# Weights in four groups in the order of need, and the first sequence's attention preparation while they arrive

## The chip, the core and the metric

The kernel runs on one core of one Trainium2 chip. The core has five engines with queues of their own: TensorE (PE), VectorE (DVE), ScalarE (ACT), GpSimd (POOL) and SyncE (SP), which here issues every DMA. They meet only at semaphores. All DMAs of a core run on the same 16 DMA engines. The metric is the device time of one execution in microseconds, lower is better; a measurement is the median of several runs.

## The reference

The input is 16 sequences of 512 tokens with 256 features. They pass four layers, each `x = x + f(layernorm(x))`: an attention, a feed-forward layer, a second attention, and a layer of decision trees. Both attentions have 16 heads of 16 features.

```
attention 0:  per key block of 256: m = max(s), e = exp(s - m); num += e @ v; den += sum(e); out = num/den; out @ w_o
ffn 0:        bitlinear(x, w): scale = clip(mean|w|, 1e-5) per output row; tern = clip(round(w/scale), -1, 1)
              forward weight = w + (tern - w), times scale
              h = bitlinear(x, w_fc) + gate * (x @ v.T @ fast_b.T @ u.T);  bitlinear(relu(h)^2, w_proj)
attention 1:  softmax(q k / 4) v with biases; out @ out_w + out_b
ffn 1:        logits = x @ W_in.T + b_in;  8 trees of 255 nodes; silu(logits) of the nodes on the path
              that the signs of the logits choose, times W_out
```

## The kernel before, in words

The sequences are worked on in 8 pairs. A pair goes through 8 phases: attention 0 of sequence 0 (phase 0) and of sequence 1 (phase 1), the feed-forward layer of both (2, 3), attention 1 of both (4, 5), and the trees of both (6, 7). Matmuls keep nearly float32 precision by splitting each factor into a high and a low float16 part and summing three products (`PRODUCTS`). So each weight is held as a high part, 64 times the weight rounded to float16, and a low part, the rest.

The order of the work is written out by hand, engine by engine, in five blocks: SP from line 260, POOL from 348, ScalarE from 471, VectorE from 659, TensorE from 963. Within a block each instruction waits for those before it. The semaphores count up over the whole kernel.

*Start-up before.* SP issues all loads (lines 262 to 265): `w_fc`, `w_proj`, small ones, the eight attention weights, `winT`, the two halves of `woutT` (127 inner nodes, 128 leaves), biases and constants; then the first two x. All of these but the last two and the x count on `w_in`, and POOL, ScalarE, VectorE and TensorE each begin with a wait for all of them (`ALL_IN`). The raw weights lie in `probs`, `oT`, `vn`, `qst` and `kst`, the buffers of attention.

- ScalarE (474 to 482): absolute values of `w_fc` and `w_proj`, a copy of the low-rank product, then the high parts of 12 weight tensors; that of `wfc` is last, since it needs the ternary weights.
- TensorE (969 to 984): means of the absolute values by matmuls with a constant, and the low-rank product.
- VectorE (662 to 707): the scales (670, 688), the ternary weights (672 to 696), ones in `vn` (698), the gated low-rank product added to `w_fc` (701), and the 12 low parts in one fused instruction each (707).

Then TensorE waits for all low parts and for `krows`, VectorE reads x, and the first sequence starts: `arrived`, `moments`, `normalise` (709 to 735), the transpositions (1004), `hT_high` and `hT_low`, `qk_unit` and `v_unit`, `qk_read`, POOL's `qk_low` (359), and SP's `stack_up` (277), 24 copies that stack high and low parts of q and k in `qst` and `kst`. Then come the row maxima of the first 7 heads (`LEAD`): a matmul into one of two PSUM banks (1040), a reduction on VectorE (753). POOL's `split_maxima` (363) cuts the maxima of four heads into three float16 parts; `maxima_rows` (1043) transposes them, `row_read` (504) copies them, and SP's `rows_up` (287) puts them as rows under q, so that the score matmul subtracts the maximum itself.

*The first attention.* In `attention_even` (1099) step s computes the scores of head s, which ScalarE exponentiates (524), and the maxima of head s + 7. In step 0 the second sequence's norm is transposed; in step 1 TensorE calls `maxima_rows(n, 1)`, which waits for POOL's `split_maxima(n, l, 1)`.

Of the kernel before, what the change touches and what calls it, by code (L numbers as in the profile page):

```python
# [55 lines left out]
def build(nc, t, out):  # L56
    ctx = ExitStack()
    with ctx:
# [84 lines left out]
        w_in = sem("w_in")  # L143
# [10 lines left out]
        w_lo = sem("w_lo")  # L154
        krows_in = sem("krows_in")
# [53 lines left out]
        loads = [  # L209
            (raw_fc, t["wfcT"].rearrange("(k p) n -> p k n", p=P)),  # L210
            (raw_pr, t["wprT"].rearrange("(k p) n -> p k n", p=P)),
            (fbs, t["fast_b"]), (uTs, t["uT"]), (vs, t["v"]), (gate[:], t["gate"]),
            (idf[:], t["idf"]), (idb[:], t["idb"].bitcast(F16)),
            *((raw_attn[:, i], w.rearrange("(k p) n -> p k n", p=P)) for i, w in enumerate(
                (t["wq0"], t["wk0"], t["wv0"], t["wo0"], t["wqkvT"][:, 0:D], t["wqkvT"][:, D:2 * D], t["wqkvT"][:, 2 * D:3 * D], t["wo1T"]))),
            (raw_in, t["winT"].rearrange("(k p) n -> p k n", p=P)),
            (raw_out[0:INNER, :, 0, :], t["woutT"].rearrange("(a n) e -> n a e", n=NODES)[0:INNER]),
            (raw_out[0:LEAVES, :, 1, :], t["woutT"].rearrange("(a n) e -> n a e", n=NODES)[INNER:NODES]),
            (bqk[:], t["bqk"]), (bv[:], t["bv"]),
            (bin_[:], t["bin"].rearrange("p (a n) -> p a n", n=2)),  # L220
            (anc[:], t["anc"].bitcast(F16)), (bo[:], t["bo"]), (thr[:], t["thr"]),
        ]
        ALL_IN = 16 * (len(loads) - PAIR)

        w_parts = [(raw_attn[:, 4 * l + i], w[l][:, HI], w[l][:, LO]) for l in range(2) for i, w in enumerate((wq, wk, wv, wo))]
        w_parts += [
# [3 lines left out]
            (raw_fc, wfc[:, HI], wfc[:, LO]),  # L230
        ]
        TERN = 18
# [28 lines left out]
        def _(sp):  # L261
            for dst, src in loads[:-PAIR]:
                sp.dma_start(dst, src).then_inc(w_in, 16)  # L263
            for q in range(PAIR):
                sp.dma_start(*loads[len(loads) - PAIR + q]).then_inc(y_out[q], 16)

# [74 lines left out]
            for q in range(PAIR):  # L341
                sp.wait_ge(y_out[q], 16 * PAIRS + 16)
# [129 lines left out]
        def _(act):  # L472
            act.wait_ge(w_in, ALL_IN)
            nc.scalar.activation(wabs, raw_fc.rearrange("p k n -> p (k n)"), ACT.Abs).then_inc(abs_done, 1)
            act.wait_ge(mean_ps, 2)
            nc.scalar.activation(wabs, raw_pr.rearrange("p k n -> p (k n)"), ACT.Abs).then_inc(abs_done, 1)
            act.wait_ge(g1_ps, 2)
            nc.scalar.activation(g1, ps[0:RANK, 4:6, :].rearrange("p a s -> p (a s)"), ACT.Copy).then_inc(g1_sb, 1)
            for i, (raw, hi, lo) in enumerate(w_parts):
                if i == len(w_parts) - 1:  # L480
                    act.wait_ge(tern, TERN)
                nc.scalar.activation(hi, raw, ACT.Copy, scale=WS).then_inc(w_hi, 1)
# [35 lines left out]
            def exps(b, ph, s, hf):  # L518
                n, g = b * NATT + ATT[ph], s // G
                act.wait_ge(exp_ps, n * (2 * H) + (2 * s + hf + 1))  # L520
                if ph == 0 and s == 4 and hf == 1:
                    for q in range(PAIR):
                        act.wait_ge(y_out[q], b * 16 + 16)
                nc.scalar.activation(probs[:, g % 2, 2 * hf:2 * hf + 2, s % G, :],  # L524
                                     ps[:, 2 + 2 * hf:4 + 2 * hf, :], ACT.Exp).then_inc(exp_rd, 1)
# [50 lines left out]

            hT_high(0, 0, 0)
            hT_high(0, 0, 1)
            qk_read(0, 0, 0)
            qk_read(0, 0, 1)  # L580
            values(0, 0, 0)
            values(0, 0, 1)
            qk_read(0, 0, 2)
            qk_read(0, 0, 3)
            row_read(0, 0)
            for b in range(PAIRS):
# [73 lines left out]
        def _(dve):  # L660
            dve.wait_ge(w_in, ALL_IN)
            nc.vector.memset(onesf, 1.0 / D).then_inc(ones_set, 1)
            nc.vector.memset(onesp, 1.0 / F0).then_inc(ones_set, 1)
            nc.vector.tensor_scalar_mul(bqk[:, 0:4:2], bqk[:, 0:4:2], QSCALE).then_inc(ones_set, 1)
            nc.vector.tensor_scalar_mul(binw[:], bin_[:], WS).then_inc(ones_set, 1)
            v3 = lambda a, k, w: a[:, 0:k * w].rearrange("p (k n) -> p k n", k=k)
            bc = lambda a, k, w: a[:, 0:w].rearrange("p (o n) -> p o n", o=1).to_broadcast([P, k, w])

            dve.wait_ge(mean_ps, 2)
            nc.vector.tensor_scalar_max(scl, ps[:, 0:2, :].rearrange("p a s -> p (a s)"), 1e-5).then_inc(tern, 1)  # L670
            dve.wait_ge(tern, 1)
            nc.vector.tensor_scalar_mul(hlf, scl, 0.5).then_inc(tern, 1)
            nc.vector.tensor_scalar_mul(nhl, scl, -0.5).then_inc(tern, 1)
            dve.wait_ge(tern, 3)
# [840 lines left out]
```

## Time and profile before

| | |
|---|---|
| median of 3 runs | 3384.36 us (3380.99 to 3385.28) |
| profiled execution | 3380.93 us, its span 3379.0 us |
| busy: PE, DVE, ACT, POOL | 3022.3, 2222.8, 1917.0, 909.1 us |
| mean granted TensorE clock | 0.944 |
| all weights in, first ScalarE work on them | 75.5 us |
| first x read by VectorE | 129.7 us |
| mean DMA rate over the span | 27 GB/s |

The span runs from the first to the last instruction; the profiled execution's own time is 1.9 us longer. A clock of 1.00 in the profile is TensorE's upper level (2.4 GHz), 0.50 the lower (1.2 GHz). Busy time of a matmul is modelled. An entry like SPq is the issue of a DMA in SP's queue, not the transfer.

### The profile page before, as it was taken

The numbers are of one execution on the slowest core, as the hardware profiler recorded it, in microseconds if no ns is written. First come the engines' busy times: TensorE is split into PE (matmuls) and PEld (weight loads), VectorE is DVE, ScalarE is ACT, GpSimd is POOL, SyncE is SP. The second block draws the span as 40 slices with busy tenths as digits, with TensorE's granted clock in tenths as the row PEclk, the third lists the DMA queues.
The fourth block names the chain that finished last, engine by engine and source line by source line (L and its number), as shares of the span: only waits on it lengthen the run. The fifth ranks groups of instructions, "written<-read, shape, count | busy, mean of one in ns | idle before, by whom it ended". The sixth has DMA issues, their size and how long they took to land.

```text
span 3379.0 us, 50607 instructions
## 1 busy us (share of the span) xinstructions
PE 3022.3 (89%) x20068; PEld 1375.3 (41%) x20068; DVE 2222.8 (66%) x4099; ACT 1917.0 (57%) x2559; POOL 909.1 (27%) x1206
## 2 busy tenths in 40 slices
PE   0488899989999899989999899998899989999899
PEld 0124255342643336333363435524254342633336
DVE  0785866758566676767667586675856667576764
ACT  0274654737547474565746566474754738456574
POOL 0013223142321414214241232314133141421413
PEclk9589899999989899998999989999899989999899
DMA  3000000000100001000010000100001000100000
GB/s 118 21 22 20 21 26 33 22 20 22 38 30 12 25 16 51 27 2 30 24 38 28 19 22 21 38 22 20 21 29 39 12 20 22 46 25 9 30 18 20
DMA packets 92700, 91.03 MB, mean 27 GB/s; under 512 B 15757, under 2 KB 89877, under 8 KB 92453
## 3 DMA queue, kind: packets, MB, share of 16 engines
q1 hardware_dynamic: 92465, 87.79, 7.6%
q8 instruction: 160, 2.62, 0.3%
q14 instruction: 75, 0.61, 0.1%
HBM read 17.48 MB, written 8.39 MB: 8 GB/s over the span
## 4 chain that ended last, share of the span: by engine, by line
PE 64%; DVE 24%; ACT 5%; SPq 3%; issue 2%; POOL 1%; DMA 1%; DVEq 0%
PE ps L995 13%; PE ps L1040 11%; PE ps L1065 10%; PE ps L1262 8%; DVE nmax L753 8%; DVE nmax L756 7%; PE ps L1020 6%; PE ps L1001 4%; PE ps L1233 3%; PE ps L1051 3%; ACT probs L524 3%; SPq L263 2%; PE ps L1008 2%; SPq L284 1%; PE ps L1253 1%
## 5 line engine op out<-in xcount | busy, mean ns | idle before, releaser
L524 ACT ACTIVATE probs<-ps 128x1024 f32<-128x1024 f32 x1024 | 1041.9, 1024 | 378.7 <-PE ps L1051 375.5
L1040 PE MATMUL ps<-kst,qst 48*128 48x512 f16 x2048 | 749.1, 409 | 145.4 <-DVE nmax L756 64.7
L753 DVE TENSOR_REDUCE nmax<-ps 128x2 f32<-128x512 f32 x1024 | 650.4, 684 | 210.9 <-PE ps L1040 204.3
L756 DVE TENSOR_REDUCE nmax<-ps 128x1 f32<-128x512 f32 x1024 | 650.3, 683 | 181.2 <-PE ps L1040 178.3
L1051 PE MATMUL ps<-qst,kst 54*128 54x512 f16 x2048 | 726.4, 406 | 5.0 <-ACT probs L524 5.0
L1065 PE MATMUL ps<-probs,vn 128*32 128x512 f32 (+1 forms) x5184 | 572.8, 515 | 6.6 <-ACT oT L512 6.6
L1040 PEld LDWEIGHTS ps<-kst,qst 48*128 48x128 f16 x2048 | 166.2, 94 | 785.0 <-DVE nmax L753 325.9
L420 POOL TENSOR_TENSOR probs<-probs 127x512 f16<-127x512 f32 (+1 forms) x256 | 292.2, 1162 | 519.7 <-ACT probs L655 519.7
L655 ACT ACTIVATE probs<-probs 127x512 f16<-127x512 f32 (+1 forms) x256 | 161.3, 630 | 350.5 <-DVE probs L949 346.8
L1262 PE MATMUL ps<-wout,probs 127*128 127x256 f16 (+1 forms) x3072 | 357.2, 273 | 0.0
L995 PE MATMUL ps<-hT,win 128*127 128x512 f16 (+1 forms) x1536 | 354.3, 380 | 2.6 <-ACT probs L631 2.6
L1262 PEld LDWEIGHTS ps<-wout,probs 127*128 127x128 f16 (+1 forms) x3072 | 297.5, 98 | 55.6 <-issue 10.7
L361 POOL TENSOR_TENSOR parts<-qk,parts 128x512 f16<-128x512 f32 x128 | 148.0, 1156 | 444.5 <-ACT qk L497 443.2
L949 DVE SCALAR_TENSOR_TENSOR probs<-ps,thr,probs 127x512 f32<-127x512 f32 (+1 forms) x256 | 179.7, 743 | 121.7 <-PE ps L1253 121.7
L367 POOL TENSOR_TENSOR npart<-nmax,zero 128x32 f16<-128x32 f32 x128 | 30.4, 238 | 793.0 <-DVE nmax L753 457.6
L995 PEld LDWEIGHTS ps<-hT,win 128*127 128x127 f16 (+1 forms) x1536 | 176.4, 117 | 162.7 <-issue 11.5
L631 ACT ACTIVATE probs<-ps,bin_ 128x512 f32<-128x512 f32 (+1 forms) x256 | 162.1, 681 | 95.1 <-PE ps L995 82.9
L1051 PEld LDWEIGHTS ps<-qst,kst 54*128 54x128 f16 x2048 | 159.5, 94 | 121.9 <-issue 79.2
L571 ACT ACTIVATE probs<-ps 128x512 f32<-128x512 f32 x128 | 76.3, 596 | 218.4 <-PE ps L995 218.2
L382 POOL TENSOR_TENSOR probs<-probs 128x512 f32<-128x512 f32 x128 | 132.6, 1039 | 221.3 <-ACT probs L571 221.3
L1065 PEld LDWEIGHTS ps<-probs,vn 128*32 128x32 f32 x5184 | 102.8, 108 | 208.8 <-issue 150.5
L995 PE MATMUL ps<-hT,wfc 128*128 128x512 f16 x768 | 184.7, 380 | 0.0
(115 smaller groups left out, 3195.9 us busy)
## 6 DMA issues: line engine op xcount, KB each, us to landing
qst<-parts SPq DMA_DIRECT2D x384, 64.0 KB, 2.6
kst<-parts SPq DMA_DIRECT2D x384, 64.0 KB, 2.6
x<-in_x SPq DMA_DIRECT2D x16, 512.0 KB, 3.6
probs<-x SPq DMA_DIRECT2D x16, 512.0 KB, 3.0
out<-probs SPq DMA_DIRECT2D x16, 512.0 KB, 3.1
qst<-nrow SPq DMA_DIRECT2D x256, 12.0 KB
qst<-in_winT SPq DMA_DIRECT2D x1, 2040.0 KB
oT<-in_wfcT SPq DMA_DIRECT2D x1, 1024.0 KB
```

The lines of the kernel that those rows point to most:

```text
L420: nc.gpsimd.tensor_tensor(mlo[0:rows, a % 2, leaf, :], masked[0:rows, a % 2, leaf, :], mhi[0:rows, a % 2, leaf, :], ALU.subtract).then_inc ...
L524: nc.scalar.activation(probs[:, g % 2, 2 * hf:2 * hf + 2, s % G, :], ps[:, 2 + 2 * hf:4 + 2 * hf, :], ACT.Exp).then_inc(exp_rd, 1)
L631: nc.scalar.activation(actv[0:rows, a % 2, leaf, :], bank[2 + leaf][0:rows], ACT.Silu, scale=1.0 / WS, bias=bin_[0:rows, a % PAR, leaf:lea ...
L753: nc.vector.tensor_reduce(nmax[:, u, 2 * tt + half, :, slot], bank[tt % 2].rearrange("p (a s) -> p a s", s=BLK), AX.X, ALU.max, negate=Tru ...
L756: nc.vector.tensor_reduce(nmax[:, u, 2 * tt + half, 0, slot:slot + 1], bank[tt % 2], AX.X, ALU.max, negate=True).then_inc(max_rd, 1)
L949: nc.vector.scalar_tensor_tensor(masked[0:rows, a % 2, leaf, :], sel_at(a, leaf)[0:rows], thr[0:rows, leaf:leaf + 1], actv[0:rows, a % 2, ...
L995: ins = mm(out_ps, w[:, a, k, col:col + width], src[:, c, k, :], start=k + i == 0, stop=k == KD - 1 and i == 2)
L1020: ins = mm(out_ps, (wq, wk)[c % 2][l][:, a, k, c // 2 * P:c // 2 * P + P], hT[ph % 2][:, d, k, :], start=k + i == 0, stop=k == KD - 1 and ...
L1040: mm(bank[tt % 2], qst[lo:hi, ai % 2, e // 2, tt * P:(tt + 1) * P], kst[lo:hi, ai % 2, e // 2, :], start=True, stop=True).then_inc(max_ps, 1)
L1051: i = mm(bank[2 + kt], kst[lo:hi, ai % 2, s // 2, kt * P:(kt + 1) * P], qst[lo:hi, ai % 2, s // 2, :], start=True, stop=True)
L1065: i = mm(bank[6][32 * j:32 * j + 32, lo:hi], vn[:, ai % 2, kt, G * g + j, :], probs[:, g % 2, kt, j, lo:hi], start=kt == 0 and 0 in halves ...
L1262: i = mm(bank[4 + tt // 2][:, tt % 2 * D:(tt % 2 + 1) * D], part[0:rows, a % 2, leaf, tt * P:(tt + 1) * P], wout[0:rows, w, c, leaf, :], s ...
```

## The change

The loads are put in four groups with a semaphore each, and x of sequence 0 comes before all of them. `first_loads`: identities and q, k, v weights of layer 0. `ffn_loads`: `w_fc`, `w_proj` and the low-rank factors. `other_loads`: the other attention weights, biases, constants. `tree_loads`: `winT` and the two `woutT`. SP issues the first group, `krows`, the second group, the first sequence's stack copies, the third group, x of sequence 1, `winT`, the first rows of maxima, and then the two `woutT`. The raw weights now lie in `probs` alone, the temporaries in `wout`, `wfc`, `hT[1]`, `oT`, `sclb` and the second sequence's half of `qst`.

The weight work is spread over the start of the first sequence. VectorE keeps the low parts of the three first weights and of `wfc`. The other eight go to POOL, which has no fused multiply and subtract here: ScalarE writes the high part and then scales the raw weight in place, POOL subtracts. Ones in `vn` are written by POOL. The diff is cut; `tern_fc` and `tern_pr` hold the old instructions of lines 669 to 684 and 686 to 704, without the memset of `vn`, and TensorE's sums are the old lines 968 to 984 with other banks.

```diff
+        attn_loads = [(raw_attn[:, i], w.rearrange(by_k, p=P)) for i, w in enumerate(names)]
+        first_loads = [(idf[:], t["idf"]), *attn_loads[0:3], (idb[:], t["idb"].bitcast(F16))]
+        ffn_loads = [(raw_fc, t["wfcT"].rearrange(by_k, p=P)), (fbs, t["fast_b"]), (uTs, t["uT"]), (vs, t["v"]), (gate[:], t["gate"]),
+                     (raw_pr, t["wprT"].rearrange(by_k, p=P))]
+        other_loads = [*attn_loads[3:], (bqk[:], t["bqk"]), (bv[:], t["bv"]), (bin_[:], t["bin"].rearrange("p (a n) -> p a n", n=2)),
+                       (anc[:], t["anc"].bitcast(F16)), (bo[:], t["bo"]), (thr[:], t["thr"])]
+        out_rows = t["woutT"].rearrange("(a n) e -> n a e", n=NODES)
+        tree_loads = [(raw_in, t["winT"].rearrange(by_k, p=P)),
+                      (raw_out[0:INNER, :, 0, :], out_rows[0:INNER]), (raw_out[0:LEAVES, :, 1, :], out_rows[INNER:NODES])]
+        OWN, FC = 3, 8
+        POOLED = len(w_parts) - OWN - 1
...
@@ SP @@
             load(0, 0)
-            load(1, 0)
-            sp.wait_ge(w_lo, len(w_parts))
+            for dst, src in first_loads:
+                sp.dma_start(dst, src).then_inc(first_in, 16)
...
+            for dst, src in ffn_loads:
+                sp.dma_start(dst, src).then_inc(ffn_in, 16)
             for c in range(4):
                 stack_up(0, 0, c)
+            for dst, src in other_loads:
+                sp.dma_start(dst, src).then_inc(attn_in, 16)
+            load(1, 0)
+            sp.dma_start(*tree_loads[0]).then_inc(tree_in, 16)
             rows_up(0, 0, 0)
+            for dst, src in tree_loads[1:]:
+                sp.dma_start(dst, src).then_inc(tree_in, 16)
@@ POOL @@
+            nc.gpsimd.memset(vn[:], 1.0).then_inc(vn_set, 1)
             pool.wait_ge(pool_set, 2)
-            pool.wait_ge(w_in, ALL_IN)
+            def weights_low(i):
+                raw, hi, lo = w_parts[i]
+                pool.wait_ge(w_hi, i + 1)
+                pool.wait_ge(w_scaled, i - OWN + (i < FC))
+                nc.gpsimd.tensor_tensor(lo, raw, hi, ALU.subtract).then_inc(w_lo_pool, 1)
...
             for c in range(4):
                 qk_low(0, c)
+            for i in range(OWN, FC):
+                weights_low(i)
             split_maxima(0, 0, 0)
             rstd_of(0, 1)
+            for i in range(FC + 1, len(w_parts)):
+                weights_low(i)
@@ ScalarE @@
+            def weights_high(i):
+                nc.scalar.activation(w_parts[i][1], w_parts[i][0], ACT.Copy, scale=WS).then_inc(w_hi, 1)
+                if i >= OWN and i != FC:
+                    nc.scalar.activation(w_parts[i][0], w_parts[i][0], ACT.Copy, scale=WS).then_inc(w_scaled, 1)
...
+                if b == 0 and ph == 0 and s == 4 and hf == 0:
+                    act.wait_ge(w_lo_pool, POOLED)
...
+            act.wait_ge(first_in, 16 * len(first_loads))
+            for i in range(OWN):
+                weights_high(i)
             hT_high(0, 0, 0)
...
             qk_read(0, 0, 3)
+            act.wait_ge(ffn_in, 16 * len(ffn_loads))
...
+            act.wait_ge(attn_in, 16 * len(other_loads))
+            for i in range(OWN, FC):
+                weights_high(i)
+            act.wait_ge(tern, TERN)
+            weights_high(FC)
             row_read(0, 0)
+            act.wait_ge(tree_in, 16 * len(tree_loads))
+            for i in range(FC + 1, len(w_parts)):
+                weights_high(i)
+            act.wait_ge(w_lo_pool, FC - OWN)
@@ VectorE @@
             normalise(0, 0)
+            for i in range(OWN):
+                weights_low(i)
             hT_low(0, 0, 0)
             hT_low(0, 0, 1)
-            for e in range(LEAD):
+            tern_fc()
+            for e in range(4):
                 maxima(0, 0, e, range(T))
+            tern_pr()
+            weights_low(FC)
+            for e in range(4, LEAD):
+                maxima(0, 0, e, range(T))
+            dve.wait_ge(attn_in, 16 * len(other_loads))
...
             arrived(0, 1)
@@ TensorE @@
+            pe.wait_ge(first_in, 16 * len(first_loads))
             transposed(0, 0, 0)
             transposed(0, 0, 1)
+            pe.wait_ge(w_lo, OWN)
...
             qk_unit(0, 0, 3)
...
             pe.wait_ge(stack[0], 16 * 4 * SLOTS)
             for e in range(LEAD):
                 for tt in range(T):
                     maxima(0, 0, e, tt, False)
                 if e == 4:
-                    pe.wait_ge(qk_sb, 4)
+                    pe.wait_ge(tern, TERN)
                     maxima_rows(0, 0)
+            pe.wait_ge(w_lo, OWN + 1)
+            pe.wait_ge(ones_set, 4)
             for b in range(PAIRS):
                 attention_even(b, 0)
+                if b == 0:
+                    pe.wait_ge(w_lo_pool, POOLED)
                 attention_odd(b, 1)
```

## Rows read from the trace of the kernel before

**Rows 1.** The page, part 1: busy time, share of the span, instructions

```profile
PE 3022.3 (89%) x20068; PEld 1375.3 (41%) x20068; DVE 2222.8 (66%) x4099; ACT 1917.0 (57%) x2559; POOL 909.1 (27%) x1206
```

**Rows 2.** Chain of waits, first 275 us, longest pieces: start, us, what

```profile
11.13 50.25 SPq L263
...
66.43 9.01 DMA anc<-in_anc
```

**Rows 3.** Line 263, one tile: duration ns min/median/max, first and last start

```profile
L263 SPq DMA_DIRECT2D kst<-in_woutT x2: 376/25312/50247, 10.7 to 11.1; - x2
```

**Rows 4.** By stretches: length, busy per engine (x instructions), PEclk, DMA share, GB/s

```profile
22.00:60.00 38.00, 0.00 (x0) 0.00 (x0) 0.00 (x0) 0.00 (x0) 0.00 (x0) 1.00 0.07 22
...
64.00:65.00 1.00, 0.00 (x0) 0.00 (x0) 0.00 (x0) 0.00 (x0) 0.00 (x0) 1.00 1.10 360
...
68.00:69.00 1.00, 0.00 (x0) 0.00 (x0) 0.00 (x0) 0.00 (x0) 0.00 (x0) 1.00 0.07 23
```

**Rows 5.** DMA issues up to 80 us: count, KB each, us to landing

```profile
kst<-in_woutT SPq DMA_DIRECT2D x1, 1024.0 KB
...
x<-in_x SPq DMA_DIRECT2D x2, 512.0 KB, 5.3
...
kst<-in_woutT SPq DMA_DIRECT2D x1, 1016.0 KB
```

**Rows 6.** Timeline of the weight work: start, us, instruction [idle before <-releaser]

```profile
75.47 1.91 ACT L474 ACTIVATE probs<-oT 128x2048 f32<-128x2048 f32 x1 [73.45 <-DMA anc<-in_anc]
...
82.86 1.22 DVE L670 TENSOR_SCALAR probs<-ps 128x1024 f32<-128x1024 f32 x1 [6.94 <-PE ps L971]
...
95.48 3.59 ACT L482 ACTIVATE win<-qst 128x4080 f16<-128x4080 f32 x1
...
98.97 3.69 ACT L482 ACTIVATE wout<-kst 127x2048 f16<-127x2048 f32 x2
...
99.17 0.75 DVE L688 TENSOR_SCALAR sclb<-ps 128x256 f32<-128x256 f32 x2
...
105.01 2.29 DVE L696 TENSOR_TENSOR wpt<-probs 128x2048 f16<-128x2048 f32 x1
...
108.22 3.47 DVE L698 MEMSET vn<- 128x4096 f32 x1 [0.92 <-DVE wpt L696]
...
111.61 2.35 DVE L701 SCALAR_TENSOR_TENSOR oT<-ps,gate,oT 128x1024 f32<-128x1024 f32 x2
```

**Rows 7.** Timeline from the norm to the mark

```profile
129.74 1.40 DVE L710 BATCH_NORM_STATS2 stats<-x 128x6 f32<-128x256 f32 x4
...
132.20 1.02 POOL L357 TENSOR_TENSOR rstd<-vpe,mhalf 128x4 f32<-128x4 f32 x1 [131.34 <-DVE vpe L729]
...
148.99 0.59 ACT L497 ACTIVATE qk<-ps 128x512 f32<-128x512 f32 x1
...
153.61 13.80 DVE L753 TENSOR_REDUCE nmax<-ps 128x2 f32<-128x512 f32 x20 [15.02 <-PE ps L1040]
...
154.79 3.77 SPq L284 DMA_DIRECT2D kst<-parts  x6
...
167.87 19.46 SPq L290 DMA_DIRECT2D qst<-nrow  x4
...
184.29 0.59 PE L1046 MATMUL ps<-idb,npart 128*24 128x128 f16 x4
```

**Rows 8.** By stretches, around the mark: columns as in rows 4

```profile
188.00:190.00 2.00, 2.00 (x6) 0.61 (x4) 0.56 (x1) 0.93 (x1) 0.00 (x0) 0.50 0.01 4
...
190.00:192.00 2.00, 1.27 (x8) 0.21 (x6) 1.30 (x3) 1.62 (x3) 0.46 (x1) 0.99 0.00 0
```

**Rows 9.** POOL by line and shape: busy us, mean ns

```profile
L361 POOL TENSOR_TENSOR parts<-qk,parts 128x512 f16<-128x512 f32 x128 | 148.0, 1156 | 444.5 <-ACT qk L497 443.2
...
L369 POOL TENSOR_TENSOR nres<-nmax,npart 128x32 f32<-128x32 f32 x128 | 32.4, 253 | 10.0
```

**Rows 10.** The page, part 3: queue, packets, MB, share of 16 engines

```profile
q8 instruction: 160, 2.62, 0.3%
```

More of the change, by code:

```diff
@@ L207, in build @@
         block = ctx.enter_context(nc.Block())
[L209 to L222, printed above, removed]
@@ L261, in _ @@
         def _(sp):
[L262 to L265, printed above, removed]
             def load(q, wrap):
@@ L341, in _ @@
             for q in range(PAIR):
-                sp.wait_ge(y_out[q], 16 * PAIRS + 16)
+                sp.wait_ge(y_out[q], 16 * PAIRS)
             for q in range(PAIR):
@@ L580, in _ @@
             qk_read(0, 0, 1)
+            act.wait_ge(vn_set, 1)
             values(0, 0, 0)
@@ L660, in _ @@
         def _(dve):
[L661 to L667, printed above, removed]
@@ L694, in _ @@
-            nc.vector.tensor_tensor(v3(tlt, M0, D), raw_pr, bc(nhl, M0, D), ALU.is_lt).then_inc(tern, 1)
-            dve.wait_ge(tern, 15)
-            nc.vector.tensor_tensor(wpt[:], v3(tgt, M0, D), v3(tlt, M0, D), ALU.subtract).then_inc(tern, 1)
-            dve.wait_ge(tern, 16)
-            nc.vector.memset(vn[:], 1.0).then_inc(vn_set, 1)
-            for k in range(KD):
-                dve.wait_ge(low_ps, 2 * (k + 1))
-                nc.vector.scalar_tensor_tensor(
-                    raw_fc[:, k, :], ps[:, [0, 6][k]:[0, 6][k] + 2, :].rearrange("p a s -> p (a s)"), gate[:, 0:1],
-                    raw_fc[:, k, :], ALU.mult, ALU.add).then_inc(tern, 1)
@@ L704, in _ @@
-            dve.wait_ge(tern, TERN)
-            for i, (raw, hi, lo) in enumerate(w_parts):
-                dve.wait_ge(w_hi, i + 1)
-                nc.vector.scalar_tensor_tensor(lo, raw, WS, hi, ALU.mult, ALU.subtract).then_inc(w_lo, 1)
             def stats_of(q, tt):
@@ new lines, in tern_pr @@
+            def tern_pr():
+                dve.wait_ge(mean_ps, 3)
+                for i in range(2):
+                    nc.vector.tensor_scalar_max(sclb[:, i, :], bank[4][:, 0:D], 1e-5).then_inc(tern, 1)
+                dve.wait_ge(tern, 11)
+                nc.vector.tensor_scalar_mul(hlf[:, 0:D], sclb[:, 0, :], 0.5).then_inc(tern, 1)
+                nc.vector.tensor_scalar_mul(nhl[:, 0:D], sclb[:, 0, :], -0.5).then_inc(tern, 1)
+                dve.wait_ge(tern, 13)
+                nc.vector.tensor_tensor(v3(tgt, M0, D), raw_pr, bc(hlf, M0, D), ALU.is_gt).then_inc(tern, 1)
+                nc.vector.tensor_tensor(v3(tlt, M0, D), raw_pr, bc(nhl, M0, D), ALU.is_lt).then_inc(tern, 1)
+                dve.wait_ge(tern, 15)
+                nc.vector.tensor_tensor(wpt[:], v3(tgt, M0, D), v3(tlt, M0, D), ALU.subtract).then_inc(tern, 1)
+                dve.wait_ge(tern, 16)
+                for k in range(KD):
+                    dve.wait_ge(low_ps, 2 * (k + 1))
+                    nc.vector.scalar_tensor_tensor(
+                        raw_fc[:, k, :], ps[:, [2, 6][k]:[2, 6][k] + 2, :].rearrange("p a s -> p (a s)"), gate[:, 0:1],
+                        raw_fc[:, k, :], ALU.mult, ALU.add).then_inc(tern, 1)
+                dve.wait_ge(tern, TERN)
@@ L847, in _, with weights_low @@
+            def weights_low(i):
+                raw, hi, lo = w_parts[i]
+                dve.wait_ge(w_hi, i + 1)
+                nc.vector.scalar_tensor_tensor(lo, raw, WS, hi, ALU.mult, ALU.subtract).then_inc(w_lo, 1)
+            nc.vector.memset(onesf, 1.0 / D).then_inc(ones_set, 1)
+            nc.vector.memset(onesp, 1.0 / F0).then_inc(ones_set, 1)
             arrived(0, 0)
@@ L1281, in _ @@
             qk_unit(0, 0, 3)
+            pe.wait_ge(ones_set, 2)
+            pe.wait_ge(abs_done, 1)
+            for j in range(2):
+                for k in range(KD):
+                    i = mm(bank[2 + j], onesf, wabs[:, k * F0 + j * S:k * F0 + (j + 1) * S], start=k == 0, stop=k == KD - 1)
+                i.then_inc(mean_ps, 1)
+            pe.wait_ge(ffn_in, 16 * len(ffn_loads))
+            for j in range(2):
+                mm(bank[j][0:RANK], fbs, uTs[:, j * S:(j + 1) * S], start=True, stop=True).then_inc(g1_ps, 1)
+            pe.wait_ge(abs_done, 2)
+            for k in range(M0):
+                i = mm(bank[4][:, 0:D], onesp, wabs[:, k * D:(k + 1) * D], start=k == 0, stop=k == M0 - 1)
+            i.then_inc(mean_ps, 1)
+            pe.wait_ge(g1_sb, 1)
+            pe.wait_ge(tern, 1)
+            pe.wait_ge(qk_sb, 4)
+            for k in range(KD):
+                for j in range(2):
+                    mm(bank[[2, 6][k] + j], vs[:, k * P:(k + 1) * P], g1[:, j * S:(j + 1) * S],
+                       start=True, stop=True).then_inc(low_ps, 1)
+            pe.wait_ge(krows_in, 32)
             pe.wait_ge(stack[0], 16 * 4 * SLOTS)
```

125 lines of the change are left out of this document (55 added, 70 removed).

## The prediction

> **What bounds the kernel now.** I read the page's busy shares first. TensorE works for 89% of the span [rows 1], so over most of it only its own work or VectorE's could be shortened. A change in the preparation is worth only what the start-up is worth, so I went on to the chain of waits of the first 275 us. There the SP queue stands for 50.25 us in one issue of line 263, and the last load of the weights lands 9.01 us after it was issued [rows 2]. The view of line 263 says which issue: of the two copies of `woutT` one took 0.38 us and the other 50.2 us [rows 3]. The table by stretches says why. From 22 to 60 us the DMA engines moved 22 GB/s at a share of 0.07, which is one engine of sixteen; at 64 to 65 us it was 360 GB/s; at 68 to 69 us again 23 [rows 4]. The copy for the inner nodes has 127 rows and 1016 KB, the one for the leaves 128 rows and 1024 KB [rows 5]. 1016 KB (1.04 MB) at 22.5 GB/s are 46 us: the copy with 127 rows ran on one engine, and the copy behind it, whose share also uses that engine, could not be issued. `anc`, also 127 rows, is the slow stretch at 68.
>
> So before, nothing computes until 75.5; then come the means, the ternary weights and all the low parts, until DVE reads x at 129.7; then norm, q/k/v, 28 maxima, and the attention. As the mark at which before and after must meet I take the second transposition of maxima (`maxima_rows(n, 1)`, in step s = 1 of the first attention), at 184.3 [rows 6, 7]. From there on both kernels issue the same work, and nothing in it depends on absolute time.
>
> **The change part by part.** The times below are those of the new kernel, in us from its start.
>
> *x first.* The pair of x landed 5.3 us after its issues [rows 5]; 512 KB at 360 GB/s are 1.5, so 2.4 of it is start and completion. Issued at 0.7, one x would be in between 4.6 and 6.0; I take 5.5. The five first loads behind it are 0.86 MB, another 2.4, before TensorE wants them. POOL now writes ones into `vn` before the first rstd: 128x4096, 3.5 us on DVE [rows 6], and 9.3 us by POOL's subtraction of 512 values in 1.16 [rows 9]. It would end between 4.3 and 10.1, and rstd wants POOL at 5.5 + (132.2 − 129.7) = 8.0 [rows 7]. I take 0, bounds 0 to 2.1. The three own low parts on DVE (about 2 us) lie under its wait for the transpositions.
>
> *Norm, q/k/v.* The same instructions as before: from stats at 129.7 to ScalarE's last copy of q/k, which ends at 149.6, is 19.9 [rows 7]. 5.5 + 19.9 = 25.4.
>
> *Ternary weights.* Abs to the first DVE instruction: 82.9 − 75.5 = 7.4; DVE from there to the projection's scale 99.2 − 82.9 = 16.3 [rows 6]. 25.4 + 23.7 = 49.1. 5.5 of the 7.4 are TensorE's sums, between the end of Abs and DVE. The clock has two levels, a factor of two apart [rows 8], so the bounds are 2.8 and 11.0; TensorE comes from q/k/v and I keep 5.5. Low-rank matmuls and the mean of the projection end before 49 and are hidden. POOL's five low parts (1.16 each [rows 9]) meet DVE's two-input instructions here; if they shut each other out, up to 5.8 more. I take 0.
>
> *Maxima and projection.* 16 maxima at 13.80/20 = 0.69 are 11.0, to 60.1 [rows 7]. `tern_pr`: 99.2 to 107.3 is 8.1, and 2.4 for the two gated adds [rows 6], to 70.6; the memset that stood between is gone. High part of `wfc` on ScalarE 1.9 (the same size as the first Abs), low part on DVE 2.3 (as `wpt`), to 74.8. ScalarE must by then have had the eleven other loads. These stand behind the 24 stack copies, whose last issue ended at 158.6 before [rows 7], here at 34.4; 11 issues of 0.63 (six took 3.77 [rows 7]) and 1.6 MB at 360 GB/s bring them in by 47. Not late.
>
> *The row of maxima, and `woutT`.* From the end of group 0's maxima (153.6 + 11.0) to SP's issue of the row at 167.87 is 3.2 [rows 7]: 78.0. Two issues later, at 79.3, SP issues the two `woutT` copies. Their shapes and their source are the same, only the buffer differs. So again 46 us on one engine, then that engine's share of the leaves, 64 KB or 2.9 us, and the 2.4 for start and completion: in at 130.6. Bounds by 22 and 23 GB/s: plus and minus 1. What SP has behind it is the rows from group 1 on, needed only at 158, and this stall of SP costs nothing. But ScalarE stands in `wait_ge(tree_in)` ahead of all exponentials. The second x, its norm and the scores of s = 0 lie beneath that wait.
>
> *Tree weights.* ScalarE writes `win` high 3.6 [rows 6], scales the source in place (the same count, 3.6), and does the same for both `wout` (3.7 and 3.7): 14.6, to 145.2, then the exponentials start. POOL can start at 130.6 + 7.2 = 137.8. Before, DVE did this in fused instructions. POOL's subtraction takes 1.16 us for 512 values and 0.25 for 32 [rows 9], so for 4080 + 2048 + 2048 values 18.5 in proportion, and 16.0 by the slope between the two with a fixed part; I take 18.5. It ends at 156.3. Only behind it in POOL's order is `split_maxima` of group 1 (four instructions of 0.25, 1.2 with the gaps), which TensorE awaits in s = 1. Mark at 157.6.
>
> *Sum.* 157.6 against 184.3: 26.7 earlier. TensorE has stood nearly all the time since about 85 and meets the mark at the lower clock level. Before, it was at 0.50 until 190 and at 0.99 after it, 6 us past the mark [rows 8]; here the same may take 6 us longer, at a loss of 0 to 4, against 0 to 2 won because DVE starts from the mark with its maxima done. I take a net loss of 1. So 26 us of the profiled execution's 3380.9 (span 3379.0 and 1.9 around it): 3355. That execution is 3.4 under the median of the runs shown; 3384.4 − 26 = 3358, which I predict.
>
> The row shows one engine for a destination in `kst`; it can't show that the new buffer leaves that so. The Trainium skill, page "DMA: Bandwidth & Descriptors", section "Why a DMA increments its semaphore by 16 and not by 1", says that the number of engines is the largest up to 16 that divides the slowest dimension of both patterns, and gives 127 partitions as 1. By that rule the buffer does not matter, the sum stays, and the first rival below would have no chance at all; the chance it gets is by the rows alone. The rule speaks against this change, which puts such a copy ahead of a wait and behind 79 us of other work.
>
> For POOL the row gives 18.5. The Trainium skill's "GPSIMD Engine Reference", section "Elementwise — side-by-side cycle accounting", has 4497 ns for a two-input operation of 2048 values; by that page, as an estimate, the three are 18.0 and the sum is 0.5 better. The row decides.
>
> **The rivals.** *The tree weights come in fast.* If the 1016 KB spread over all engines in their new place, both copies are in 5.8 us after they start, at 360 GB/s [rows 4]: `tree_in` at 87.5, POOL from 94.7 to 113.2, mark at 114.5, 69 us won, 3315. For it: only the destination's kind was seen before. Against: count and source row length are unchanged, and `anc`, in another buffer, also ran at 23 GB/s.
>
> *The one engine is shared.* Before, nothing computed while it ran, in 22 to 60. Now it runs beside maxima, norm and the start of attention, whose instructions are fetched over the same DMA engines. At half the rate it takes 46 us more: mark at 204, 20 us lost, 3404. It decides from 26 us on, that is from 14.4 GB/s down (slower by the bound from 33 us on, 13 GB/s). Against: the larger of the instruction queues carries 2.62 MB in the entire span [rows 10], under 1 GB/s. The Trainium skill (same DMA page, section "Queues, rings and completion order") has each engine take turns between its rings packet by packet, which is how this would happen; no row here shows it.
>
> *The work ahead of `woutT` stretches.* Everything before 79.3 moves the end one for one. If hand-overs between four engines, the lower clock and DVE against POOL together cost 16 us or more, the gain is under 10: about 3375. It is not the same as the change not doing what it says, though near it: the norm really starts 124 us earlier, but only 26 of them arrive, since `woutT` stands behind.
>
> **How the numbers follow.** The forecast has 0.80; its own bounds: what lies before 79.3 minus 4 to plus 7 (parts of the bounds above, which will not all be reached), one engine and POOL minus 3 to plus 1, clock minus 2 to plus 3, and 2 for the median: 3346 to 3371. The fast tree load has 0.09, the stretched start 0.07, the shared engine 0.04. The fast case (3315) may stay outside, with part of the others: I give 3344 to 3372, which leaves out some 0.2. A measurement of this kernel tells no change within about 0.2%, 7 us. Faster by more: 0.80, 0.09 and 0.05 of the stretched case: 0.94. Within: 0.02. Slower: 0.04.
>
> **What would show it.** Right: first stats near 5.5; SP issues `woutT` near 79, and DMA then runs at 22 GB/s for 46 us; ScalarE's idle time before the high part of `win` is about 50 us and ends near 131 on `woutT`; POOL's three long subtractions last some 18.5 us and end near 156; the mark is at 158. Wrong: a `woutT` at hundreds of GB/s, an issue of it well off 79, POOL at another rate per value, or a second attention that needs longer than before from the mark on.

## The result and the profile after

The changed kernel takes 3352.93 us (median of 4, 3352.20 to 3355.05) against 3384.22 (median of 4); the ratio is 0.991, 95% interval 0.9893 to 0.9927. The profiled execution is 3353.39 us with a span of 3351.6, against 3380.93 and 3379.0: 27.5 us less in the profiles, 31.3 in the medians. 3358 was predicted, with a range of 3344 to 3372.

TensorE's row of busy time answers to [rows 1]. Its work is the same within 6 us, its share rose by one point.

```profile
PE 3017.0 (90%) x20068; PEld 1373.4 (41%) x20068; DVE 2210.2 (66%) x4090; ACT 1927.8 (58%) x2567; POOL 938.7 (28%) x1215
```

The timeline answers to [rows 6] and [rows 7]: the start of the first sequence with the ternary work between (start, us, instruction, idle before and what ended it). VectorE reads x at 4.5 and not at 129.7. ScalarE's last copy of q/k ends at 23.8, the maxima start at 48.3, the projection's scale at 59.2, the low part of `wfc` ends at 74.2. The last row is the issue of both `woutT` copies, at 79.0; one of them again blocks SP for 42 us.

```profile
4.51 1.41 DVE L703 BATCH_NORM_STATS2 stats<-x 128x6 f32<-128x256 f32 x4 [3.38 <-DMA x<-in_x]
...
23.20 0.59 ACT L517 ACTIVATE qk<-ps 128x512 f32<-128x512 f32 x1
...
45.24 3.13 DVE L859 TENSOR_TENSOR probs<-probs,oT 128x2048 f32<-128x2048 f32 x1
...
48.29 11.02 DVE L746 TENSOR_REDUCE nmax<-ps 128x2 f32<-128x512 f32 x16
...
59.22 0.75 DVE L864 TENSOR_SCALAR sclb<-ps 128x256 f32<-128x256 f32 x2
...
71.96 2.29 DVE L884 SCALAR_TENSOR_TENSOR wfc<-probs,wfc 128x2048 f16<-128x2048 f32 x1 [2.06 <-ACT wfc L500]
...
77.30 1.68 SPq L300 DMA_DIRECT2D qst<-nrow  x2
...
79.02 42.95 SPq L323 DMA_DIRECT2D probs<-in_woutT  x2
```

The stretches show where the gain stops (columns as in [rows 4]). From 82 to 120 us DMA moves 22 GB/s at a share of 0.07, while the busy times of those 38 us are 4.67 for PE, 7.49 for DVE, 0 for ACT and 1.02 for POOL. The leaves come at 358 GB/s, then the one engine catches up on its share of them. The last three rows belong to the clock: it is at 0.50 until 162 and full from 164, 7 us past the mark; in [rows 8] it was 6.

```profile
82.00:120.00 38.00, 4.67 (x17) 2.04 (x17) 7.49 (x24) 0.00 (x0) 1.02 (x1) 0.50 0.07 22
...
124.00:126.00 2.00, 0.00 (x0) 0.00 (x0) 0.00 (x0) 0.00 (x0) 0.00 (x0) 0.50 1.09 358
...
128.00:130.00 2.00, 0.00 (x0) 0.00 (x0) 0.00 (x0) 0.00 (x0) 0.00 (x0) 0.50 0.07 22
...
160.00:162.00 2.00, 2.00 (x6) 0.57 (x4) 0.36 (x1) 0.72 (x1) 0.00 (x0) 0.50 0.01 2
162.00:164.00 2.00, 1.64 (x7) 0.22 (x6) 1.12 (x2) 1.66 (x3) 0.49 (x1) 0.70 0.00 0
164.00:166.00 2.00, 1.79 (x12) 0.65 (x12) 1.37 (x3) 1.39 (x2) 0.66 (x1) 1.00 0.28 98
```

The chain of waits names the two pieces that stand where 50.25 us of SP stood in [rows 2]. The profile gives the first to an unknown queue; the idle time of ScalarE in the next fence says that it ended on `woutT`.

```profile
77.27 54.70 another core or an unknown queue
...
147.11 8.09 POOL wout L375 x2
```

The stretch from that wait to the mark: ScalarE's tree weights (131.99 to 146.2), POOL's three subtractions (7.93 and 8.09, to 155.2), `split_maxima` behind them, and TensorE's second transposition of maxima, the mark, at 156.5.

```profile
131.99 3.60 ACT L500 ACTIVATE win<-probs 128x4080 f16<-128x4080 f32 x1 [54.72 <-DMA probs<-in_woutT]
...
139.23 7.93 POOL L375 TENSOR_TENSOR win<-probs,win 128x4080 f16<-128x4080 f32 x1 [53.09 <-ACT probs L502]
...
144.40 1.90 ACT L502 ACTIVATE probs<-probs 128x2048 f32<-128x2048 f32 x1
...
147.11 8.09 POOL L375 TENSOR_TENSOR wout<-probs,wout 127x2048 f16<-127x2048 f32 x2
...
156.12 0.25 POOL L395 TENSOR_TENSOR npart<-nres,npart 128x32 f16<-128x32 f32 x1
...
156.52 0.58 PE L1075 MATMUL ps<-idb,npart 128*24 128x128 f16 x4 [7.26 <-POOL npart L395]
```

### The profile page after: what moved, and what is told of

Same layout as the page of the kernel before. It is cut to its first block, busy times and chain, and to the rows that moved or that the text cites. A ratio compares the mean times of both kernels' runs of the same rounds, so it can differ in the third digit from the quotient of the medians.

```text
span 3351.6 us, 50628 instructions
## 1 busy us (share of the span) xinstructions
PE 3017.0 (90%) x20068; PEld 1373.4 (41%) x20068; DVE 2210.2 (66%) x4090; ACT 1927.8 (58%) x2567; POOL 938.7 (28%) x1215
## 4 chain that ended last, share of the span: by engine, by line
PE 64%; DVE 23%; ACT 6%; issue 2%; another core or an unknown queue 2%; SPq 2%; POOL 2%; DMA 0%; DVEq 0%; POOLq 0%
PE ps L1024 13%; PE ps L1069 11%; PE ps L1094 10%; PE ps L1291 8%; DVE nmax L746 8%; DVE nmax L749 7%; PE ps L1049 6%; PE ps L1030 5%; PE ps L1262 3%; PE ps L1080 3%; ACT probs L546 3%; PE ps L1037 2%; SPq L294 1%; PE ps L1282 1%
```

## The experiments

Each time is the median of a kernel's runs, and each ratio is to the kernel before, run beside it on the same chip. The kernel before took 3384.2 us beside the changed kernel, 3382.3 beside e1 to e4, 3381.4 beside e5 to e8 and 3382.6 beside e9. So up to 3 us of a difference between rows of different groups need not come from the edit. "Trees in" is the first ScalarE work behind the wait for all tree weights (for all weights in the kernel before and e2); e6, e7 and e9 have no such single wait. "Mark" is the second transposition of maxima, as in the prediction. The last column is the span of the profiled execution less its mark. The diffs of e4, e6 and e9 are cut.

| kernel | trees in | mark | median (lowest to highest) | ratio to before, 95% | span − mark |
|---|---|---|---|---|---|
| before | 75.5 | 184.3 | 3384.2 | | 3194.7 |
| changed | 132.0 | 156.5 | 3352.9 (3352.2 to 3355.1) | 0.9893 to 0.9927 | 3195.1 |
| e1_split | 88.3 | 112.8 | 3311.9 (3304.0 to 3312.4) | 0.9775 to 0.9805 | 3189.4 |
| e2_before_split | 32.4 | 141.2 | 3337.9 (3337.6 to 3340.3) | 0.9858 to 0.9891 | 3194.5 |
| e3_124 | 101.5 | 126.0 | 3323.0 (3321.1 to 3324.7) | 0.9814 to 0.9843 | 3194.8 |
| e4_dve_low | 132.5 | 151.3 | 3347.3 (3345.0 to 3349.9) | 0.9886 to 0.9915 | 3191.8 |
| e5_order | 101.0 | 125.5 | 3322.3 (3316.3 to 3322.8) | 0.9811 to 0.9838 | 3195.1 |
| e6_early | | 101.0 | 3298.5 (3294.4 to 3299.5) | 0.9743 to 0.9770 | 3194.9 |
| e7_early_norm | | 94.9 | 3293.0 (3290.2 to 3294.9) | 0.9728 to 0.9754 | 3196.8 |
| e8_no_overlap | 130.6 | 155.1 | 3345.9 (one execution) | | 3189.0 |
| e9_ports | | 89.6 | 3286.8 (3278.8 to 3289.0) | 0.9699 to 0.9725 | 3195.7 |

**e1_split: the tree weights over many engines.**

```diff
-                      (raw_out[0:INNER, :, 0, :], out_rows[0:INNER]), ...
+                      (raw_out[0:112, :, 0, :], out_rows[0:112]), (raw_out[112:INNER, :, 0, :], out_rows[112:INNER]), ...
```

> The changed kernel, with the 127 rows of the inner nodes loaded by two copies of 112 and 15 rows, so that they run on 16 and 15 DMA engines. My theory: the exponentials of the first attention wait for woutT, which runs on one engine for 46 us. With it on many engines the tree weights are in 2.1 MB / 360 GB/s = 5.8 us after the start, near 88 instead of 132, and all behind them is 44 us earlier: 3353 - 44 = 3309 us. Rival (another wait right behind takes its place, the low parts ahead or DVE): under 10 us won, 3343 or more.

Stretches and timeline of this run: `woutT` moves at 284 and 348 GB/s (159 in the slowest microsecond between them), ScalarE starts on `win` at 88.31 (expected near 88), and the mark is at 112.8.

```profile
81.00:82.00 1.00, 0.07 (x2) 0.10 (x4) 1.00 (x5) 0.00 (x0) 0.00 (x0) 0.50 1.14 284
...
86.00:87.00 1.00, 0.00 (x0) 0.00 (x0) 1.00 (x3) 0.00 (x0) 0.00 (x0) 0.50 1.09 348
```

```profile
88.31 3.60 ACT L500 ACTIVATE win<-probs 128x4080 f16<-128x4080 f32 x1 [12.03 <-DMA probs<-in_woutT]
...
112.82 0.59 PE L1075 MATMUL ps<-idb,npart 128*24 128x128 f16 x4 [7.25 <-POOL npart L395]
```

The mark is 43.7 us earlier, the median 41.1 us (3311.9; 3309 expected). The wait for `woutT` was on the path with its whole length, and nothing took its place. The rival (3343 or more) is out.

**e2_before_split: the same edit in the kernel before.**

> The kernel before, with the same split of the inner rows and nothing else. The one engine stood from about 20 to 66 us there too: ScalarE should start on the weights near 31 instead of 75.5, and the time should be 3384 - 44 = 3340 us, less than the changed kernel's 3353. My theory has the change and the split as independent: the change only moved the stall behind the first sequence's preparation, so the distance from this kernel to the changed one with the split is again about 31 us. Rival: the change earns its time by hiding the slow load, so once the load is quick little is left, and this kernel is within 10 us of the changed one with the split (3309 to 3319).

In this timeline ScalarE starts at 32.4 in place of 75.5. The second fence is the mark.

```profile
32.38 1.91 ACT L475 ACTIVATE probs<-oT 128x2048 f32<-128x2048 f32 x1 [30.36 <-DMA anc<-in_anc]
```

```profile
141.15 0.59 PE L1047 MATMUL ps<-idb,npart 128*24 128x128 f16 x4
```

The mark is 43.1 us earlier and the time 3337.9, which is 44 us below the kernel before run beside it. One split copy wins more than the whole change does (31). The change with the split is 26.0 us below this kernel (5 less than expected, 28.3 by the marks), where the rival gave under 10. So the change did not earn its 31 us by hiding the slow copy. It paid for that copy in full, as the kernel before did, and earned them with the rest of the start-up.

**e3_124: four engines.**

```diff
-                      (raw_out[0:INNER, :, 0, :], out_rows[0:INNER]), ...
+                      (raw_out[0:124, :, 0, :], out_rows[0:124]), (raw_out[124:INNER, :, 0, :], out_rows[124:INNER]), ...
```

> The changed kernel, with the inner rows in two copies of 124 and 3 rows. By the Trainium skill (DMA: Bandwidth & Descriptors, Why a DMA increments its semaphore by 16 and not by 1) 124 rows give 4 engines, since 4 is the largest divisor up to 16. As an estimate by that page: 992 KB on 4 engines of 22.5 GB/s are 11.3 us, tree weights in near 96, 36 us won, 3317. Rival: a count that is no multiple of 16 falls to one engine: 992 KB take 45 us, 22 GB/s in the table by stretches, and the time stays near 3352.

In the stretches the share is 0.27, four engines and not one.

```profile
84.00:86.00 2.00, 0.00 (x0) 0.00 (x0) 0.80 (x6) 0.00 (x0) 1.02 (x1) 0.50 0.27 65
...
98.00:99.00 1.00, 0.00 (x0) 0.00 (x0) 0.00 (x0) 0.00 (x0) 0.00 (x0) 0.50 0.27 90
```

```profile
101.50 3.60 ACT L500 ACTIVATE win<-probs 128x4080 f16<-128x4080 f32 x1 [24.65 <-DMA probs<-in_woutT]
...
126.03 0.58 PE L1075 MATMUL ps<-idb,npart 128*24 128x128 f16 x4 [7.27 <-POOL npart L395]
```

The number of engines is as the rule of the Trainium skill ("DMA: Bandwidth & Descriptors", "Why a DMA increments its semaphore by 16 and not by 1") has it, and the rival (one engine, 3352) is out. The size was off: four engines moved 65 to 67 GB/s, 16 each and not 22.5, from 82 to 88 us, and the weights came in at 101.5 and not 96; the time is 3323 and not 3317. At 98 us, in the tail of the transfer, four engines moved 90 GB/s, 22.5 each. So the low rate does not come from the number of engines alone; its cause is open.

**e4_dve_low: the tree weights' low parts on VectorE.**

```diff
@@ POOL, before the pairs @@
-            for i in range(FC + 1, len(w_parts)):
-                weights_low(i)
@@ VectorE @@
             normalise(0, 1)
+            for i in range(FC + 1, len(w_parts)):
+                weights_low(i)
@@ ScalarE, weights_high @@
-                if i >= OWN and i != FC:
+                if OWN <= i < FC:
```

> The changed kernel, with the three low parts of the tree weights on VectorE in the old fused form, so that ScalarE doesn't scale these sources and POOL doesn't subtract. My theory: behind woutT the path is ScalarE and POOL up to the second transposition of maxima at 156.5. Now it is ScalarE's first high part (3.6, to 135.6), DVE 4.4 + 2.2 + 2.2 to 144.4, four maxima, the scores and the exponentials of step 0: mark near 149, 7 us won, 3346. Rival (POOL's part hides behind ScalarE's work, and the exponentials set the mark): nothing won, 3353.

VectorE's three low parts end at 144.9; the four maxima of head 7 and the scores of step 0 stand behind them, and ScalarE's second half of step 0 waits.

```profile
136.14 4.41 DVE L883 SCALAR_TENSOR_TENSOR win<-probs,win 128x4080 f16<-128x4080 f32 x1 [48.19 <-ACT win L499]
139.61 1.00 ACT L545 ACTIVATE probs<-ps 128x1024 f32<-128x1024 f32 x1
140.46 4.49 DVE L883 SCALAR_TENSOR_TENSOR wout<-probs,wout 127x2048 f16<-127x2048 f32 x2
144.87 2.67 DVE L745 TENSOR_REDUCE nmax<-ps 128x2 f32<-128x512 f32 x4
...
151.27 0.58 PE L1076 MATMUL ps<-idb,npart 128*24 128x128 f16 x4
```

The mark is at 151.3, 5.2 us earlier (7 expected), although the trees came in 0.5 us later. The median is 3347.3, 5.6 us lower; with each taken against the kernel before run beside it, the gain over the changed kernel is 3.7, which by itself is not clear of the noise. By the marks POOL's subtractions were on the path, so the rival is out. From the end of the low parts to the mark it is 6.4 us and not 4.6: the maxima, scores and transpositions of step 0, which had lain under the wait and beside POOL's subtractions, now come one after another behind the low parts.

**e5_order: `woutT` issued at 41 us, still on one engine.**

```diff
-            rows_up(0, 0, 0)
             for dst, src in tree_loads[1:]:
                 sp.dma_start(dst, src).then_inc(tree_in, 16)
+            rows_up(0, 0, 0)
```

> The changed kernel, with both woutT copies issued right after winT, near 40.5 us, and the row of the first maxima behind them; woutT still runs on one engine. My theory: what counts is when woutT is issued. It comes in 38 us earlier, near 93; SP stands in the issue until 83, so the row goes up 6 us late and lands behind woutT on the same engine, near 93 to 96, but ScalarE is busy with the tree weights until 107 anyway. Mark (second transposition of maxima) near 118, 38 us won, 3315. Rival: the blocked SP queue holds up the row and with it the scores, and the order of issue is there for that; then the first exponentials come only after the row, at least 15 us are lost again and the time is 3330 or more.

```profile
40.86 49.82 SPq L322 DMA_DIRECT2D probs<-in_woutT  x2
...
100.97 3.60 ACT L500 ACTIVATE win<-probs 128x4080 f16<-128x4080 f32 x1 [25.07 <-DMA probs<-in_woutT]
```

```profile
44.00:46.00 2.00, 0.00 (x0) 0.00 (x0) 1.97 (x2) 2.00 (x5) 1.27 (x1) 0.50 1.00 410
...
48.00:50.00 2.00, 1.81 (x4) 0.30 (x3) 1.79 (x4) 0.74 (x2) 2.00 (x3) 0.50 0.06 22
```

SP stands for 49.8 us and puts the row up 13 us late. `woutT` is issued at 41, but in the stretches all engines are full (410 GB/s) until 48 with `winT` before it, and only then does the one engine's rate stand alone; I had not counted that. The trees are in at 101.0 (93 expected), the mark at 125.5 (118), the time is 3322.3. It is 30.6 us below the changed kernel, and above 3315 as well as below 3330. The first scores did come late, but mark less "trees in" is 24.5 us, as in the changed kernel (24.5), e1 (24.5) and e3 (24.5). So the late row cost nothing, and the mechanism is mine; the time at which `woutT` gets its engine was mis-sized.

**e8_no_overlap: POOL's five low parts moved off VectorE's ternary work.**

```diff
             act.wait_ge(attn_in, 16 * len(other_loads))
+            act.wait_ge(tern, 9)
             for i in range(OWN, FC):
```

> The changed kernel, with ScalarE waiting for VectorE's last instruction on w_fc (the product with the scale) before it makes the attention weights' high parts, so that POOL's five low parts run beside one-input maxima and no longer beside two-input VectorE work. In the changed kernel that last product took 3.13 us, 2.29 alone, and POOL's first two 1.92 and 3.20, 1.16 alone. My theory (the two engines hinder one another only when both read two tiles): the product takes 2.29, POOL's five 1.16 each, woutT is issued 0.8 us earlier. Rival (the long ones come from something else, such as ScalarE writing the same tiles): they stay long beside the maxima.

POOL's first subtractions in the changed kernel, then the same place in this run:

```profile
44.30 1.92 POOL L375 TENSOR_TENSOR wo<-probs,wo 128x512 f16<-128x512 f32 x1 [19.27 <-ACT probs L502]
...
46.18 3.20 POOL L375 TENSOR_TENSOR wq<-probs,wq 128x512 f16<-128x512 f32 x1
```

```profile
44.58 2.29 DVE L860 TENSOR_TENSOR probs<-probs,oT 128x2048 f32<-128x2048 f32 x1
...
48.25 1.16 POOL L375 TENSOR_TENSOR wo<-probs,wo 128x512 f16<-128x512 f32 x1 [22.19 <-ACT probs L502]
...
77.51 43.01 SPq L323 DMA_DIRECT2D probs<-in_woutT  x2
```

VectorE's product takes 2.29 (3.13 in the changed kernel) and POOL's subtractions 1.16, beside maxima. `woutT` is issued 1.5 us earlier (0.8 expected), the mark comes 1.4 us earlier (155.1). Only 0.8 of this is the collision: VectorE's work was already 0.7 us ahead at its first ternary instruction (30.48 against 31.14) and at this product (44.58 against 45.24), before the edit could act. The product's start lies between 44.1 and 46.1 in the other versions. One execution, 3345.9 us; it is shorter than that explains, since it also took 6 us less after the mark.

In e5 the collision went the other way. Its code is that of the changed kernel up to here, but VectorE's product began 0.02 us before POOL's first subtraction. The product kept its 2.29 us and the subtraction took 3.29:

```profile
44.71 2.29 DVE L859 TENSOR_TENSOR probs<-probs,oT 128x2048 f32<-128x2048 f32 x1
44.73 3.29 POOL L375 TENSOR_TENSOR wo<-probs,wo 128x512 f16<-128x512 f32 x1 [18.53 <-ACT probs L502]
```

**e6_early and e7_early_norm: the tree weights out of the wait, the second norm into idle time.**

```diff
@@ SP @@
-            sp.dma_start(*tree_loads[0]).then_inc(tree_in, 16)
+            sp.dma_start(*tree_loads[0]).then_inc(win_in, 16)
-            rows_up(0, 0, 0)
             for dst, src in tree_loads[1:]:
                 sp.dma_start(dst, src).then_inc(tree_in, 16)
+            rows_up(0, 0, 0)
@@ ScalarE: win now stands before wfc in w_parts, FC = 9 @@
+            act.wait_ge(win_in, 16)
+            weights_high(FC - 1)
             act.wait_ge(tern, TERN)
             weights_high(FC)
+            weights_high(FC + 1)
             row_read(0, 0)
+            weights_high(FC + 2)
```

> The changed kernel with the split of the inner rows, all of woutT issued near 41 us, and the high part of win made in ScalarE's idle time before the ternary weights are ready, those of wout around the first row of maxima; POOL's low parts accordingly, ahead of the second rstd. My theory: after the split the path is ScalarE's 14.6 us and POOL behind it. With these out of the way DVE's first 28 maxima and the second sequence's norm set the mark, as before the change: DVE's second stats at 82, mark 11 us later at 93 against 112.8 with the split alone: 20 us won on it, 3292. Rival: POOL's 8 us for win meet DVE's two-input work of the projection's ternary weights and slow both, as at 45 us, and 5 us or more of it are lost: 3297 or more.

e7 besides loads x of sequence 1 behind `krows` and calls `arrived(0, 1)`, `moments(0, 1)`, `normalise(0, 1)` before `tern_fc()`.

> As the run before, and the second sequence's x is loaded behind the first group and its norm is taken on DVE in the idle time between 13 and 31 us. DVE's 5.4 us of norm leave the path: mark at 88, 5 us won on the run before, 3287. Rival: the rstd ahead of POOL's first low part of q and the longer DVE chain delay the first sequence by as much as they save: no difference.

The timeline of e6: POOL's subtraction for `win` runs from 57.05 to 64.95. VectorE's scaling of 256 values, 0.29 us elsewhere, starts at 59.23 and ends at 65.09. Then VectorE's two-input comparison runs from 65.37, and POOL's cast of 32 values, 0.24 elsewhere, takes 2.17.

```profile
57.05 7.90 POOL L376 TENSOR_TENSOR win<-probs,win 128x4080 f16<-128x4080 f32 x1 [5.09 <-ACT probs L503]
...
59.23 5.86 DVE L869 TENSOR_SCALAR oT<-sclb 128x256 f32<-128x256 f32 x1
...
65.37 2.29 DVE L872 TENSOR_TENSOR wout<-probs,oT 128x2048 f32<-128x2048 f32 x1
65.60 2.17 POOL L394 TENSOR_TENSOR npart<-nres,zero 128x32 f16<-128x32 f32 x1
```

```profile
54.82 7.90 POOL L376 TENSOR_TENSOR win<-probs,win 128x4080 f16<-128x4080 f32 x1 [1.72 <-ACT probs L503]
...
60.36 2.51 DVE L869 TENSOR_SCALAR oT<-sclb 128x256 f32<-128x256 f32 x1
...
85.21 2.49 DVE L909 TENSOR_SCALAR bqk<-bqk 128x2 f32<-128x2 f32 x1
```

e6's mark is at 101.0 and its time 3298.5 (93 and 3292 expected); its rival, 5 us or more lost to POOL beside VectorE, is what happened: 5.6 us there, and 2.3 more in the scaling of `bqk`. e7 gains 5.5 us on it (5 expected); its mark of 94.9 and its time of 3293.0 miss the expected 88 and 3287 by what e6 had already lost. Of that loss it keeps 2.2 and 2.3.

**e9_ports: POOL's long work beside maxima only.** The edit is shown against e7.

```diff
@@ SP @@
+            sp.dma_start(*tree_loads[0]).then_inc(win_in, 16)
             for dst, src in other_loads:
                 sp.dma_start(dst, src).then_inc(attn_in, 16)
-            sp.dma_start(*tree_loads[0]).then_inc(win_in, 16)
@@ POOL: win stands first behind the three own weights in w_parts @@
-            for i in range(OWN, FC):
+            pool.wait_ge(ones_set, 4)
+            for i in range(OWN, OWN + 3):
                 weights_low(i)
             split_maxima(0, 0, 0)
+            pool.wait_ge(tern, TERN)
+            for i in range(OWN + 3, FC):
+                weights_low(i)
@@ VectorE: the scaling of bqk and bin_ comes here @@
             tern_fc()
+            dve.wait_ge(attn_in, 16 * len(other_loads))
```

> As the run with the second norm early, with POOL's long work put where VectorE reads one tile only: winT is loaded ahead of the third group, POOL subtracts win and two attention weights beside the 16 maxima (it waits for VectorE's ternary work on w_fc and the two small scalings, which come forward), and the other three after the ternary work of the projection. Theory: VectorE and POOL shut one another out for whole instructions when VectorE reads two SBUF tiles or scales one in SBUF; in the run before that cost VectorE 0.8 (3.13 for 2.29), 2.2 (2.51 for 0.29) and 2.3 (2.49 for 0.16). Without them the mark comes 5.4 us earlier, at 89.5, and the time is 3288. Rival: these stretches are not on the path, since POOL's own later subtractions and ScalarE set the mark; then the mark stays near 95 and the time at 3293.

```profile
48.44 11.02 DVE L752 TENSOR_REDUCE nmax<-ps 128x2 f32<-128x512 f32 x16
...
49.03 7.91 POOL L375 TENSOR_TENSOR win<-probs,win 128x4080 f16<-128x4080 f32 x1 [23.18 <-ACT probs L506]
...
60.15 0.29 DVE L872 TENSOR_SCALAR oT<-sclb 128x256 f32<-128x256 f32 x1
...
89.56 0.58 PE L1081 MATMUL ps<-idb,npart 128*24 128x128 f16 x4
```

Mark at 89.6 (89.5 expected), 3286.8 us (3288 expected). VectorE's maxima took 0.69 each beside POOL's 7.91 us, its scaling 0.29. The rival, a mark that stays near 95, is out. One short collision is left: VectorE's low part of `wfc` took 2.44 in place of 2.29, and a subtraction of POOL beside it 3.21 in place of 1.16. This is the best version: 95.8 us below the kernel before run beside it, and 66 below the changed one.

## Why the prediction was right

Its steps against the profile after, in us from the start:

| step | predicted | measured |
|---|---|---|
| first stats | 5.5 | 4.5 |
| last copy of q/k ends | 25.4 | 23.8 |
| first maxima | 49.1 | 48.3 |
| projection's scale | 60.1 | 59.2 |
| low part of `wfc` ends | 74.8 | 74.2 |
| `woutT` issued | 79.3 | 79.0 |
| tree weights in | 130.6 | 132.0 |
| ScalarE's tree weights end | 145.2 | 146.2 |
| POOL's three subtractions, their end | 18.5, 156.3 | 16.0, 155.2 |
| mark | 157.6 | 156.5 |
| from the mark to the end | 1 more | 0.4 more |

- *One engine.* The copy of 127 rows ran on one engine in the new buffer too; e1 and e3 show that this is set by the count of rows, and e1 and e2 that it costs the changed kernel 44 us and the one before 43. From issue to landing it took 53 us, 1.7 more than the sum. The stall of SP behind it cost nothing, as said: SP was free again at 122.0, and its next row of maxima went up only at 157.75.
- *The wait that takes the place of the old one.* It was named in its place: ScalarE idles 54.7 us before the high part of `win`. That is shown by e1.
- *POOL.* The term was mis-sized: 18.5 in proportion, 16.0 measured, which is the other end given (a fixed part and 1.9 us per 1000 values). The Trainium skill's 4.5 us for a two-input operation of 2048 values ("GPSIMD Engine Reference") was 4.05 here. e4 shows that the term is on the path.
- *POOL against VectorE.* Taken as 0 with a bound of 5.8: the product took 0.8 longer, and nothing longer in e5, where VectorE began first. So the choice was near, by luck in part: which engine begins first was a matter of tenths of a microsecond here. As a mechanism it was underrated: in e6 such collisions cost 7.9.
- *The clock.* The feared 6 us more at the lower level were 1: full clock 7 us past the mark against 6.
- *The rivals.* The fast tree load did not occur in the changed kernel, but the time it was given (3315) is what e1 measured, 3312. The shared engine did not occur: 22 GB/s, and 23 in e5 from 52 to 90 us, where VectorE worked for 29.6 of the 38 us. The stretched start did not occur either.
- *Errors that cancel.* The issue of `woutT` was 0.3 early, the copy 1.7 long, POOL 2.5 short; together they give the mark's 1.1. So the sum is nearer than its terms. The bounds of the forecast, added up, give 3347 to 3371 and not 3346 to 3371, which changes nothing.
- *The median.* It fell by 31.3 us against the 27.5 of the profiles, and 26 predicted. From the mark to the end the profiled executions took 3189.0 to 3196.8 us, with no relation to the edits that I can see, and e1's own four executions spread over 8.4 us. So the 4 us between median and profiles can be chance; the interval of the ratio holds both.

## What to carry to other kernels

Before hiding a slow load, look at what makes it slow: here a DMA share of one sixteenth in the stretches came from a count of rows, 127, that has no divisor up to 16 but 1, and splitting it into 112 and 15 won more than rebuilding the start. A reordered start is worth the time at which its last wait ends, so follow every moved load to the instruction that waits for it and to what that engine does next. Work moved to an idle POOL is not free by itself: look at what VectorE does at that time. In these runs maxima out of PSUM kept their time beside POOL; instructions with two SBUF tiles, and scalings of a single one, waited for POOL or held it up.

## What the runs showed that was not expected

- VectorE and POOL excluded one another for whole instructions, in both directions, where VectorE read two SBUF tiles or scaled one in SBUF, and the one that began first ran at full speed: a 0.29 us scaling in SBUF took 5.86 and ended 0.14 us after POOL's (e6), a 0.24 us POOL operation took 2.17 beside a two-input comparison, while 16 maxima, which read PSUM, kept 0.69 us each beside POOL (e9). It agrees with the Trainium skill, "SBUF — State Buffer", section "Who interferes with whom", which calls it an exclusive lock on a shared port pair and names VectorE instructions with two SBUF inputs, and `tensor_scalar` among those that can take the whole pair.
- The issue of a copy behind one that ran on a single engine held SP for 42 to 50 us, while the DMA share was 0.07 (the kernel before, the changed one, e5). Behind four engines (e3) it was 9.4, and with the split (e1) no issue took more than 0.6.
- Four engines of a transfer moved 16 GB/s each and one alone 22 (e3, and the changed kernel), but four moved 22.5 each in e3's last microseconds.
- The same work from the mark on differs by up to 8 us between executions.
